# Indirect transfers of 128 rows instead of 125, and a reordered last pipeline, in a four-layer graph network kernel

## The reference

```
x1 = norm(x + L0(x))         # batch norm, softmax-weighted sum of relu(hn[src]+edge_attr) over the edges of each dst, W1, layer norm, W2
x2 = norm(x1 + relu(bn((x1 + sum over edges of x1[src]) @ w1 ...)))      # GIN: needs means over all nodes
x3 = norm(x2 + softplus-net(sum over edges of (x2[src] @ W_in2f) * filter(edge_attr_20)))
out = norm(x3 + mean@W2l.T + h@W2r.T),  h = relu(mean over edges of x3[src] @ W1l.T + x3 @ W1r.T),  mean = mean over edges of h[src]
```

## Time and profile before

| | us |
|---|---|
| median of three runs | 2369.95 |
| the profiled execution | 2367.93 |
| its span (first to last instruction) | 2366.2 |
| busy: PE / DVE / ACT / POOL | 2088.3 / 1990.5 / 1785.1 / 1525.5 |

### The profile page before, as it was taken

One profiled execution on the slowest core, in us unless ns is written; L12 is line 12 of the kernel. 1 busy time (PEld: TensorE's weight loads), 2 busy tenths in 40 slices (PEclk: granted clock), 3 DMA queues, 4 the chain that ended last, 5 costly groups with the idle time before them and its releaser, 6 DMA issues. The chain is left out here.

```text
span 2366.2 us, 45653 instructions
## 1 busy us (share of the span) xinstructions
PE 2088.3 (88%) x14016; PEld 1742.7 (74%) x14016; DVE 1990.5 (84%) x2942; ACT 1785.1 (75%) x3691; POOL 1525.5 (64%) x1114
## 2 busy tenths in 40 slices
PE   5999999999999899997999788888699999686663
PEld 4999999999998677775776677777577776564553
DVE  7999999999997566666998799999699999696553
ACT  4889998989987577775776688888699998574221
POOL 6888866777740543440687788880178886788887
PEclk9999999999999899998999899999899999898776
DMA  4767665555665798886786788885377776686553
GB/s 112 158 160 161 158 165 170 163 161 157 180 196 174 204 258 251 255 254 181 199 215 139 168 195 197 194 201 159 101 201 192 199 218 185 162 221 164 147 160 89
DMA packets 322547, 427.40 MB, mean 181 GB/s; under 512 B 113683, under 2 KB 169589, under 8 KB 322308
## 3 DMA queue, kind: packets, MB, share of 16 engines
q1 hardware_dynamic: 210004, 367.20, 54.7%
q0 software_dynamic: 112000, 56.93, 14.1%
q10 hardware_dynamic: 304, 0.36, 0.0%
HBM read 239.24 MB, written 185.90 MB: 180 GB/s over the span
## 5 line engine op out<-in xcount | busy, mean ns | idle before, releaser
L1814 POOL DMA_INDIRECT acc<-combined,first_ x100 | 211.5, 2115 | 84.9 <-issue 37.3
L515 PE MATMUL banks<-mats,g_hT 128*125 128x256 f32 x1000 | 260.6, 383 | 0.0
L534 PE MATMUL banks<-mats,g_zT 128*125 128x128 f32 x2000 | 238.8, 273 | 0.0
L860 POOL DMA_INDIRECT gin_xs<-x,from_ x100 | 126.2, 1262 | 161.0 <-DMA x_of_src<-gin_xs 135.2
L534 PEld LDWEIGHTS banks<-mats,g_zT 128*125 128x125 f32 x2000 | 228.2, 188 | 0.0
L1876 POOL DMA_INDIRECT em_y<-acc,from_ x100 | 134.0, 1340 | 129.5 <-PE banks L2018 99.6
L515 PEld LDWEIGHTS banks<-mats,g_hT 128*125 128x125 f32 x1000 | 190.5, 190 | 28.8 <-issue 0.4
L1035 DVE TENSOR_TENSOR gin_acc<-gin_acc,gin_qr 125x512 f32<-125x512 f32 x125 | 86.6, 693 | 119.3 <-ACT gin_qr L995 119.3
L595 ACT ACTIVATE g_zT<-banks,cols 128x500 f32<-128x500 f32 x250 | 179.1, 776 | 2.6 <-PE banks L523 2.6
L578 ACT ACTIVATE g_sq<-banks 125x512 f32<-125x512 f32 x250 | 144.9, 590 | 43.3 <-PE banks L515 42.5
L438 POOL DMA_INDIRECT g_xd<-in_x,idx x100 | 124.3, 1243 | 71.2 <-PE banks L549 44.4
(11 more groups left out here) (411 smaller groups left out, 6615.5 us busy)
## 6 DMA issues: line engine op xcount, KB each, us to landing
acc<-g_zero SPq DMA_DIRECT2D x126, 224.0 KB
x<-g_x SPq DMA_DIRECT2D x125, 224.0 KB
g_x<-in_xT SPq DMA_DIRECT2D x100, 250.0 KB
h<-gin_hr SPq DMA_DIRECT2D x50, 448.0 KB
al_h<-h SPq DMA_DIRECT2D x38, 448.0 KB
al_x<-x SPq DMA_DIRECT2D x38, 448.0 KB
out<-al_out SPq DMA_DIRECT2D x38, 448.0 KB
gin_x<-x SPq DMA_DIRECT2D x37, 448.0 KB
```

What stands on the lines that cost most here:

```text
L515: m = nc.tensor.matmul(bank[0:P, 256 * j:256 * j + 256], HT[q % 2][:, c:c + P], K.W1c, start=False, stop=j == 1)
L534: m = nc.tensor.matmul(pO[q % 2][0:P, D * j:D * j + D], ZT[q % 2][:, h, P * j:P * j + P], K.W2[:, h, :], start=False, stop=j == R - 1 and ...
L1814: pool.indirect_dma_start(out=K.acc, out_offset=bass.IndirectOffsetOnAxis(ap=K.first[:, g, r:r + 1], axis=0), in_=CR[:, g, r * D:r * D + D ...
```

## The change

1. All index tables get 128 partitions. The three new partitions hold harmless rows: source row 0 for gathers, a number past the bound for scatters that skip, and twelve spare rows behind `acc` for the scatter that adds. All eleven kinds of indirect DMA move 128 rows instead of 125, and the buffers that they fill or read have 128 partitions.
2. For that: in `setup` one more iota on POOL and two more memsets on DVE; at the end of `gen_all` one more small DMA that clears the spare rows; in `edges_first` one more matmul before the first tile; in `edges_last` three memsets on DVE before the late nodes.
3. The last pipeline: PE calls `second` one tile later, DVE and ACT have another order.
4. `XD`, `HTD` and `IV` have five buffers each (the new ones are parts of `CR`); SP issues the loads of tiles 0 and 1 before the last three stores of late nodes and those of tiles 2 to 4 before the last one, after a wait for the late nodes' use of these parts of `CR`.

```diff
+PAD = 128 - P
-    idx = keep("idx", [P, 3, EG, R], I32)
+    idx = keep("idx", [128, 3, EG, R], I32)
+                nc.gpsimd.iota(K.first_all[:, :, :], pattern=[[0, EG], [PAD, R]], base=N + E + G - P, channel_multiplier=1).then_inc(slots, 1)
+                link(nc.vector.memset(K.of_h3_all[:, :, :], 0))
+                link(nc.vector.memset(K.to_d_all[:, :, :], NOWHERE))
+                sp.dma_start(K.acc[N + E + G:N + E + G + R * PAD, :], zero[0:R * PAD, 0:D]).then_inc(cleared, 16)
+                    if k == 0:
+                        nc.tensor.matmul(pC[:, :], K.ones3[:, :], K.bias_y[:, :], start=True, stop=True)
...
-        pool.indirect_dma_start(out=K.acc, out_offset=bass.IndirectOffsetOnAxis(ap=K.first[:, g, r:r + 1], axis=0),
-                                in_=CR[:, g, r * D:r * D + D], in_offset=None, compute_op=ALU.add).then_inc(added, 16)
+        pool.indirect_dma_start(out=K.acc, out_offset=bass.IndirectOffsetOnAxis(ap=K.first_all[:, g, r:r + 1], axis=0),
+                                in_=CR_all[:, g, r * D:r * D + D], in_offset=None, compute_op=ALU.add).then_inc(added, 16)
...
-        H, XD = sb("h", [P, R, D], k=NH), sb("xd", [P, R, D]) + [ends.XD]
+        H, XD = sb("h", [128, R, D], k=NH), sb("xd", [P, R, D]) + [ends.XD, ends.rows(0), ends.rows(1)]
+        IV = sb("iv", [128, G]) + [ends.cols(s) for s in (4, 5, 6)]
+        HTD = sb("hdT", [128, G], k=3) + [ends.cols(s) for s in (2, 3)]
...
                 def load(k):
-                    past(sp, c, k - 3)
-                    past(sp, cs, k - 3)
-                    past(sp, me, k - 2)
+                    past(sp, c, k - 5)
+                    past(sp, cs, k - 5)
+                    past(sp, me, k - 5)
...
                         n.store(sp, i - 5)
-                for k in range(EG):
+                    if i == LATE + 1:
+                        load(0)
+                        load(1)
+                    if i == LATE + 3:
+                        past(sp, n.a, 2 * LATE - 1)
+                        past(sp, n.hT, 2 * LATE - 1)
+                        for k in range(2, 5):
+                            load(k)
+                for k in range(5, EG):
                     load(k)
...
-                steps(EG, [(0, turn), (0, second)])
+                steps(EG, [(0, turn), (1, second)])
...
-                steps(EG, [(1, lambda k: norm.square(act, k, flat(C[k % 3]), c)), (0, copy), (1, norm.log_of(act)),
+                steps(EG, [(0, copy), (1, lambda k: norm.square(act, k, flat(C[k % 3])[0:P, :], c)), (1, norm.log_of(act)),
...
+                for i in range(3):
+                    nc.vector.memset(C[i][:, :, :], 0.0).then_inc(blank, 1)
...
-                steps(EG, [(1, residual), (1, norm.reduce_of(dve)), (0, sums), (1, apply), (0, average)])
+                steps(EG, [(1, residual), (0, sums), (1, norm.reduce_of(dve)), (0, average), (1, apply)])
```

More of the change, by code:

```diff
@@ L149, in setup @@
     K.b2c, K.b1s, K.b1d = [keep(n, [128, 1]) for n in ("b2c", "b1s", "b1d")]
-    idx = keep("idx", [P, 3, EG, R], I32)
-    K.src, K.dst, nxt = idx[:, 0], idx[:, 1], idx[:, 2]
-    K.from_, K.first, K.of_h3, K.to_d, K.slot = [keep(n, [P, EG, R], I32) for n in ("from_", "first_", "of_h3", "to_d", "d_slot")]
+    idx = keep("idx", [128, 3, EG, R], I32)
+    K.src_all, K.dst_all, nxt = idx[:, 0], idx[:, 1], idx[0:P, 2]
+    K.from_all, K.first_all, K.of_h3_all, K.to_d_all, K.slot_all = [keep(n, [128, EG, R], I32) for n in (
+        "from_", "first_", "of_h3", "to_d", "d_slot")]
+    K.src, K.dst, K.from_, K.first, K.of_h3, K.to_d, K.slot = [t[0:P] for t in (
+        K.src_all, K.dst_all, K.from_all, K.first_all, K.of_h3_all, K.to_d_all, K.slot_all)]
     K.c = lambda n: K.cols[:, K.col[n]:K.col[n] + 1]
@@ L881, in keep @@
                         past_slot(sp, got, g, 16 * R)
-                        move(sp, slots_of(K.xs1, g), flat(XS[g % 4]), kept[g % 4])
+                        move(sp, slots_of(K.xs1, g), flat(XS[g % 4])[0:P, :], kept[g % 4])
                 def store(q):
@@ L1580, in _ @@
                     past(pool, added, k - 1, 16 * R)
-                    sum_round(pool, K, CR, last - k, added)
+                    sum_round(pool, K, CR_all, last - k, added)
                     if k >= 1:
-                        h_rows(pool, K, CR, last - k + 1, got_h)
+                        h_rows(pool, K, CR_all, last - k + 1, got_h)
                 past(pool, added, rounds - 1, 16 * R)
@@ L1851, with __init__, sb @@
 class Inputs:
-    def __init__(self, nc, K, CR, ctx):
-        def sb(n, k):
-            return [ctx.enter_context(nc.sbuf_tensor(f"em_{n}{i}", [P, R, D], F32)) for i in range(k)]
-        self.K, self.CR = K, CR
-        self.X, self.XD, self.YD, self.Y = sb("x", 2), sb("xd", 3), sb("yd", 3), sb("y", 4)
+    def __init__(self, nc, K, CR_all, ctx):
+        def sb(n, k, rows=P):
+            return [ctx.enter_context(nc.sbuf_tensor(f"em_{n}{i}", [rows, R, D], F32)) for i in range(k)]
+        self.K, self.CR = K, CR_all[0:P]
+        self.X, self.XD, self.YD, self.Y_all = sb("x", 2), sb("xd", 3), sb("yd", 3), sb("y", 4, 128)
+        self.Y = [y[0:P] for y in self.Y_all]
         self.IV = [ctx.enter_context(nc.sbuf_tensor(f"em_iv{i}", [128, G], F32)) for i in range(3)]
@@ L1890, in __init__, with rows, cols @@
         self.H[1], self.X[0] = self.X[0], self.H[1]
-        self.XD = CR[:, EG - 1, :].rearrange("p (r d) -> p r d", r=R)
+        self.XD = self.CR[:, EG - 1, :].rearrange("p (r d) -> p r d", r=R)
     def pair(self, s):
         return self.CR[:, s:s + 2, :].rearrange("p s (r d) -> p (s r) d", r=R)
+    def rows(self, s):
+        return self.CR[:, s, :].rearrange("p (r d) -> p r d", r=R)
+    def cols(self, s):
+        return self.CR_all[:, s, 0:G]
     def load(self, sp, n):
@@ L1902, in put @@
         for r in range(R):
-            pool.indirect_dma_start(out=self.out, out_offset=bass.IndirectOffsetOnAxis(ap=self.K.first[:, k, r:r + 1], axis=0),
-                                    in_=self.CR[:, k, r * D:r * D + D], in_offset=None, bounds_check=N - 1,
+            pool.indirect_dma_start(out=self.out, out_offset=bass.IndirectOffsetOnAxis(ap=self.K.first_all[:, k, r:r + 1], axis=0),
+                                    in_=self.CR_all[:, k, r * D:r * D + D], in_offset=None, bounds_check=N - 1,
                                     oob_is_err=False).then_inc(self.sent[k % 4], 16)
@@ L2368, in second @@
                     for j in range(R):
-                        nc.tensor.matmul(pC[k % 2][0:P, D * j:D * j + D], HTD[k % 3][:, P * j:P * j + P], K.W("W2rT"), start=False, stop=False)
+                        nc.tensor.matmul(pC[k % 2][0:P, D * j:D * j + D], HTD[k % 5][:, P * j:P * j + P], K.W("W2rT"), start=False, stop=False)
                     past(pe, me, k)
@@ L2453, in program @@
         big = ExitStack()
-        CR = big.enter_context(nc.sbuf_tensor("combined", [P, EG, R * D], F32))
+        CR_all = big.enter_context(nc.sbuf_tensor("combined", [128, EG, R * D], F32))
         ROUNDS, PAIRS = 10, NG // 2 - LATE
         got_h = K.lasting("h_got", 1)[0]
-        edges_first(nc, K, CR, ROUNDS, got_h)
+        edges_first(nc, K, CR_all, ROUNDS, got_h)
         K.end_phase()
         inputs = ExitStack()
-        ins, ends = Inputs(nc, K, CR, inputs), Ends(nc, K, CR, out)
-        side, ahead = sums_and_gather(K, CR, ROUNDS, sem("added"), got_h, ins)
+        ins, ends = Inputs(nc, K, CR_all, inputs), Ends(nc, K, CR_all, out)
+        side, ahead = sums_and_gather(K, CR_all, ROUNDS, sem("added"), got_h, ins)
         nodes_alone(nc, K, out, PAIRS, side, ahead)
```

94 lines of the change are left out of this document (48 added, 46 removed).

## The result

The changed kernel takes 2338.22 us (median of 4 runs, 2336.59 to 2339.19) beside 2369.87 for the kernel before on the same chip: ratio 0.9864, 95% interval 0.985 to 0.9878. In a later group of runs it took 2339.66 beside 2372.22, ratio 0.9866 (0.9851 to 0.9881). It is faster by 1.4%, as forecast in sign and inside the range of 2303 to 2371, but the point forecast, 2329, was 9 us too low. The profiled execution took 2339.05 us with a span of 2337.3.

What follows compares the result with a forecast made beforehand. POOL's 204 DMA instructions in a row were taken to bound the last stretch. Scatters from 2180.3 plus 138.2 end at 2318.5; + 6.2 - 0.3 + 0.4 = 2324.8 span, + 1.7 and 2.0 to the median: 2329 us, range 2303 to 2371.

Steps and rivals of the forecast that it cites:

- The bound: Last stretch: POOL's 204 DMA instructions in a row fill the last 341 us; in earlier stretches POOL has room.
- A DMA's price: POOL's indirect DMAs at 128 rows: a gather takes 1.00 us at its shortest, 0.205 less for each gather or scatter.
- the lengthened ones: Last stretch: POOL DMAs above their floor, 19.6 us over 100 gathers and 10.0 over 100 scatters, put down to DVE and kept.
- The reading behind the lower bounds: POOL's DMA time: the adding scatter's extra 0.752 us read as 400 more writes of 1.9 ns, giving 0.69 us for 128 moves.
- the rival "nothing": POOL's DMA time is mostly fixed, so 128 rows save nothing there: 2369 us, chance 0.12.
- The phases before, nothing: Stretches before the last: shorter POOL DMAs gain nothing, since POOL's slack covers them.
- The last pipeline's start: With early loads the means follow the scan, the first tile is ready at 2180.3, and scatters start then instead of 2201.3.
- The twelve early load issues: SP's loads ahead of the last late store: at most 12.5 us of issuing, taken as 0 (0 to 5).
- Pace: Last pipeline: POOL asks for a tile every 5.53 us; the compute loop of 5.47 or 4.54 us just keeps up.
- The tail: Span's end after the last scatter: 6.2 us of landing and ending kept from the old kernel, less 0.3 for quicker landing.
- "Compute becomes the bound": Last pipeline: POOL's DMA falls to 0.69 us and compute sets the pace: 2313 us, 2303 at high clock, chance 0.16.
- "slower": Sixteen engines cost POOL more than five, 1.39 us per DMA in the last two phases: 2425 us, chance 0.14.

Runs made afterwards that it cites:

- the first experiment: The changed kernel with all eleven kinds of indirect DMA back at 125 rows, its new last pipeline kept: 2374.39 us, ratio 1.0026.

## Why the prediction was right, and where it was 9 us off

**The bound.** Right. The end was POOL's row of DMAs, and only the last stretch paid.

**A DMA's price.** Right in size, from bounds far apart. The forecast took 1.00 us as the floor of a gather and 0.205 less for each DMA; the floor is 0.941, and the means fell by 0.237 (gather) and 0.182 (scatter). Over 100 of each that is 41.9 us for the 41 of the sum. Keeping the lengthened ones as DVE's was right too: 24 gathers and 24 scatters start under a DVE instruction with both operands in SBUF and average 1.81 and 1.47 us, the other 76 of each 0.96 and 0.99. The count of moves, 144, came out exactly. The reading behind the lower bounds (a fixed price per move, from the adding scatter) did not hold: two thirds of the moves went and 22% of the time. The adding scatter fell by 0.405 us, the gather by 0.264; both are far from the rival "nothing". By the Trainium skill's rule that spoke for that rival ("DMA: Bandwidth & Descriptors", "Anatomy of one DMA — SWDGE (gpsimd) path") the time would have stayed at 2369; 0.264 us on every gather do not agree with it.

**The phases before, nothing.** Nearly right in the sum: the last phase begins 0.5 us later, 0.3 of it the setup, for which I had put down 0.4. That hides what cancels. POOL's cost did end on a path in one of them, the middle stage: its closing drain is the last thing there in both kernels (2021.9 us before, where the other engines are done at 2018.1). It ends 7.6 us behind POOL's last scatter with 128 rows and 4.6 with 125; the last scatter itself ends 2.2 us sooner. The first big stage takes 757.8 us for 754.9, and the next four are 0.3 to 1.0 us shorter each. In the first one DVE's shift of `x` (it adds a column named `half`) became longer; from 170 to 400 us it is, before and then after:

```profile
L673 DVE TENSOR_SCALAR g_x<-g_x,half 128x500 f32<-128x500 f32 x31 | 14.7, 474 | 0.0
```

```profile
L681 DVE TENSOR_SCALAR g_x<-g_x,half 128x500 f32<-128x500 f32 x31 | 17.4, 560 | 0.0
```

That is 2.7 us in this stretch and 4.8 over the whole stage (49.0 and 53.8 us for all 100). With 125 rows and the new pipeline (the first experiment) it is 473 ns, so it comes with the 128 rows. Over the stage, the instances with no POOL DMA beside them last 472 ns on average in the changed kernel and 473 before, those with one 549 and 492. In size this can be the loss of 2.8 us; that it is was not tried. DVE is busy for 99% of this stretch, but PE, with 229.7 of 230 us before and 228.5 after, is as close to the bound.

**The last pipeline's start.** The chain of durations was right and its origin wrong. From the end of the last blend the first tile took 7.7 us (2176.4 to 2184.1), against 7.9 forecast (2172.4 to 2180.3). What failed is the tacit step that the late nodes would end where they did: their end came 4.0 us later, 3.5 of it in this phase, and of these 3.0 by the first blend. (In the second profile of the same kernel the first blend is as late, but the last ends 2.0 us later in its phase than before, not 3.5.) That put the tile at 2184.1. The other part is a term that I put at nothing: from a tile's end to POOL's scatter pass 0.9 us, which the kernel before does not show at its first scatter, since the tile was waiting there. So the scatters start at 2185.1 for 2180.3. The twelve early load issues, priced at 0 to 5, cost 0 to 0.4.

**Pace.** Right in sign: POOL sets it and compute keeps up. POOL's stretch of scatters took 140.4 us for 138.2, since scatters gained 0.182 instead of 0.205. The compute loop was priced too high: 5.47 or 4.54 us, where 4.25 was seen at the upper clock in the first tiles and 4.29 held over 25 tiles in the run with three scatters. One round of it in the changed kernel (granted clock 1.00):

```profile
2185.06 0.69 DVE L2439 TENSOR_TENSOR el_c<-el_xd,banks 125x512 f32<-125x512 f32 x1 [0.95 <-PE banks L2399]
2185.66 1.25 DVE L2425 TENSOR_TENSOR_SCAN el_sum<-same,el_sum,el_hT 128x500 f32<-128x500 bf16 x1
2186.84 0.66 DVE L1176 TENSOR_REDUCE el_n_s<-el_n_sq 125x4 f32<-125x512 f32 x1
2187.41 0.67 DVE L2432 TENSOR_TENSOR el_me<-el_sum,combined 128x500 f32<-128x500 f32 x1
...
2189.31 0.69 DVE L2439 TENSOR_TENSOR el_c<-combined,banks 125x512 f32<-125x512 f32 x1 [0.53 <-PE banks L2399]
```

Means to residual takes 1.90 us, just what I had priced for the short products (2.84 - 0.93). The difference is in the other three: I had added up their durations, but each starts about 0.1 us before the one ahead of it has ended (0.60 + 1.18 + 0.57 for 0.69 + 1.25 + 0.69).

**The tail.** This is the step that failed most. It was 6.2 - 0.3 = 5.9 us in the forecast and 11.8 in the trace. I took it over from the old kernel as a lump of landing and ending, and priced the only part I thought would change, the landing (from the last scatter's end to the drain it fell from 2.1 to 1.4). The drain, 3.0 of the old 6.2 us, has a row of its own in the trace of before and none in my account. It became 9.2.

The account closes: scatters start 4.8 later, last 2.2 longer, tail 5.9 longer, less the 0.4 that the sum had put aside for the setup, are 12.5 us, the difference of the spans (2337.3 - 2324.8). The time itself was off by 9 only because its median lies 0.8 us below the profiled execution, where I had added 2.0 for before's.

**The rivals.** "Compute becomes the bound" did not come about, with POOL at 0.94 instead of 0.69; it is what happens with 128 rows in the old order, where tiles came every 6.31 us. (The low end of that rival, 2303, comes to 2302 when its sum is done again.) "Nothing" and "slower" fall with the floors.

## What to carry to other kernels

Ask of an indirect DMA first how many rows its busiest engine gets: 127 rows cost this POOL 2.54 us, 125 cost 1.21, 128 cost 0.94. Padding to a count that sixteen divides paid here only where POOL stood on the path, and most of it only once what lay directly under it was shortened too: the two parts change the time by +0.26% and -0.36% alone and by -1.36% together. And take the tail of a span apart, drain by drain, before carrying it over: a term that nobody has opened can change as well.

## What the runs showed of the hardware that was not expected

- POOL's closing drain took 2.99 us behind 125-row DMAs and 9.20 behind 128-row ones, which are quicker to issue and leave fewer packets (352 for the last eleven, 32 each, instead of 80). Behind a recent drain it took 0.05 us, with the last landing already waited for.
- A gather of 127 rows holds POOL for 2.54 us, one of 126 for 0.99; 64 rows on all sixteen engines save only 84 ns of 984.
- DVE's 128x500 `TENSOR_SCALAR` on `g_x` lasts 474 ns beside 125-row DMAs and 560 beside 128-row ones in the same stretch, while the 128x500 `TENSOR_TENSOR` and scan rows next to it moved by 2% at most and the other 128x500 `TENSOR_SCALAR`, on `g_ms`, stayed at 412 and 409.
- A POOL DMA is lengthened when it starts under a DVE instruction with both operands in SBUF. Under a 125x1024 `TENSOR_TENSOR` of that kind one took 1.83 us on average before (34 of them) and 1.70 after (49); under a `TENSOR_REDUCE` of 125x1024, which reads one operand, 1.22 and 0.96, near the floors.
